# Graph attention on one core: slots of tile and row block in place of padded blocks, and 28 tiles fetched row by row by SyncE

## The reference

```
messages = x[col]
g = (messages @ W_gate.T + b_gate)[:, 0]
h = messages @ W_lin.T + b_lin
seg_max = segment_max(g, row)
e = exp(g - seg_max[row])
denom = segment_sum(e, row) + 1e-16
pooled = segment_sum((e / denom[row])[:, None] * h, row)
out = layernorm(x + pooled @ W_out.T + b_out)
```

## Time and profile before

| what | value |
|---|---|
| median of three runs | 2772.81 us |
| the profiled execution | 2774.84 us |
| its span, first to last instruction | 2773.0 us |
| mean granted TensorE clock | 0.604 of full speed |
| instructions | 24,827 |
| PE, DVE, ACT, POOL busy | 945.0, 1669.9, 147.0, 1746.0 us |

### The profile page before, as it was taken

How to read it: one execution, slowest core, us unless ns; L and a number is a source line. 1 busy time by engine, 2 the same in 40 slices (tenths; PEclk the granted TensorE clock), 3 DMA queues, 4 the chain that set the end, 5 groups by cost and what they waited for, 6 DMA issues and landing times.

```text
span 2773.0 us, 24827 instructions
## 1 busy us (share of the span) xinstructions
PE 945.0 (34%) x4932; PEld 799.1 (29%) x4932; DVE 1669.9 (60%) x5579; ACT 147.0 (5%) x489; POOL 1746.0 (63%) x1795
## 2 busy tenths in 40 slices
PE   6322110243342432433423424334234243342340
PEld 5311110232242332422423323323223233232230
DVE  9999997365464564654645646546455465464466
ACT  2311110000000000000000000000000000000006
POOL 0010004777777777777777777777777777777737
PEclk9655555566555565565656656556565565565665
DMA  3220002222222222222222222222222222222563
GB/s 121 95 80 0 0 0 55 54 54 54 54 54 55 54 55 54 54 55 54 54 55 54 55 54 54 55 54 54 55 55 55 54 54 55 54 54 55 47 29 93
DMA packets 91152, 148.65 MB, mean 54 GB/s; under 512 B 30551, under 2 KB 62127, under 8 KB 90495
## 3 DMA queue, kind: packets, MB, share of 16 engines
q0 software_dynamic: 56224, 117.06, 19.5%
q1 hardware_dynamic: 34032, 31.04, 3.3%
q10 hardware_dynamic: 864, 0.20, 0.1%
HBM read 134.35 MB, written 13.83 MB: 53 GB/s over the span
## 4 chain that ended last, share of the span: by engine, by line
POOL 33%; DVE 27%; issue 23%; PE 8%; DVEq 4%; DMA 3%; ACT 1%; ACTq 0%; POOLq 0%; SPq 0%
POOL arena L354 33%; DVE spread L875 5%; DVE nodes_sb L881 4%; PE bank L574 4%; DMA arena<-node_table,gather_at 3%; DVE rows_a L709 2%; DVEq L903 2%; DVE rows_b L710 2%; DVE rows_a L710 2%; DVE rows_b L709 2%; DVE turn_b L710 1%; PE bank L487 1%; DVE turn_b L709 1%; DVE turn_a L710 1%; DVE turn_a L709 1%
## 5 line engine op out<-in xcount | busy, mean ns | idle before, releaser
L354 POOL DMA_INDIRECT arena<-node_table,gather_at x1757 | 1681.0, 957 | 829.7 <-issue 527.2
L574 PE MATMUL bank<-arena,spread 128*128 128x129 f32 x3520 | 738.4, 379 | 323.3 <-DVE nodes_sb L881 220.2
L574 PEld LDWEIGHTS bank<-arena,spread 128*128 128x128 f32 x3520 | 643.4, 276 | 413.8 <-DVE nodes_sb L881 291.4
L875 DVE TENSOR_SCALAR spread<-iota_row,place_t,weights 128x128 f32<-128x128 f32 x1760 | 596.6, 355 | 174.0 <-PE bank L574 73.3
L881 DVE SCALAR_TENSOR_TENSOR nodes_sb<-nodes_sb,weights,bank 128x129 f32 x1760 | 605.4, 344 | 56.4 <-PE bank L574 11.2
L853 DVE TENSOR_TENSOR_SCAN run_max<-pen,bank 40x128 f32<-40x128 f32 (+1 forms) x45 | 18.5, 412 | 752.5 <-PE bank L556 752.5
L556 PE MATMUL bank<-ident,arena 128*40 128x128 f32 (+1 forms) x45 | 17.1, 380 | 703.2 <-DMA arena<-node_table,gather_at 703.2
L556 PEld LDWEIGHTS bank<-ident,arena 128*40 128x40 f32 (+1 forms) x45 | 5.3, 118 | 711.2 <-issue 711.2
L543 PE MATMUL bank<-ident,dst_f 40*128 40x40 f32 x44 | 13.1, 297 | 269.6 <-DVEq L684 269.6
L543 PEld LDWEIGHTS bank<-ident,dst_f 40*128 40x128 f32 x44 | 7.9, 179 | 279.3 <-issue 279.3
L533 PE MATMUL bank<-ident,rows_a 128*128 128x128 f32 x112 | 28.1, 428 | 153.2 <-DVE rows_a L735 117.9
(11 more groups left out here) (151 smaller groups left out, 993.0 us busy)
## 6 DMA issues: line engine op xcount, KB each, us to landing
arena<-node_table,gather_at POOLq DMA_INDIRECT x1757, 19.8
node_table<-arena SPq DMA_DIRECT2D x1, 6347.7 KB
nodes_sb<-in_x SPq DMA_DIRECT2D x4, 1562.5 KB
arena<-in_x SPq DMA_DIRECT2D x12, 448.0 KB
out<-arena SPq DMA_DIRECT2D x12, 448.0 KB
k<-sorted_keys SPq DMA_DIRECT2D x132, 20.0 KB
turn_a<-in_src SPq DMA_DIRECT2D x1, 828.0 KB
turn_b<-in_dst SPq DMA_DIRECT2D x1, 828.0 KB
```

What stands on the lines that cost most here:

```text
L354: pool.indirect_dma_start(out=gathered_rows[par][:, t, :], out_offset=None, in_=table[:, :], in_offset=bass.IndirectOffsetOnAxis(ap=gather ...
L574: last = pe.matmul(tile_ps(slot), lhsT=spread[:, slot, :], rhs=gathered_rows[par][:, b * BATCH + u, 0:WIDTH], start=True, stop=True)
L875: return dve.tensor_scalar(spread[:, slot, :], iota_row[:, :], place_t[par][:, t:t + 1], weights[par][:, 0, t:t + 1], ALU.is_equal, ALU.mult)
```

## The change

- **No padding.** The keys hold row and fetched node, and are sorted as they are: 1661 tiles (42 chunks, the last of 21 tiles). A tile may now span blocks. A **slot** is a pair of a tile and a block that it touches: 1661 + 97 = 1758 slots, in 44 rounds of 40. The counting, the one-hots and the pad keys go.
- **Tables ordered by PE.** Which tile a slot belongs to follows from counting how many tiles' ends lie before it: `find_ended` compares on DVE, PE sums over partitions, `place_slots` makes one-hot rows `chosen` and the register tables `pe_at` and `dve_at`, and PE multiplies `row_f` and `drop_x` of the last four chunks by `chosen` (`choose_rows`, `choose_drops`). Rows in a slot that belong to another block find no place and give zeros.
- **Weights on ACT.** `spread` holds only ones and zeros; ACT scales each fetched row by its weight, 40 instructions a chunk. PE takes the tile at an address from a register.
- **Ring.** Five chunk buffers, not two, since a round may still need a tile of three chunks before. All loops are written out.
- **SP fetches.** In chunks with c % 3 < 2, tile 32 is fetched by SP: 128 transfers of one row (28 such tiles). POOL leaves them out and issues 1633.
- **Moved.** The linear bias goes into the table by a bias matmul a batch. The copy of `blank_row` becomes `memset(sums, 0.0)`. x is loaded late, into sort buffers and two ring buffers, and POOL adds the bias behind its last gather. The constant 1e-16 is added before the reciprocal. The first two batches of spreads of a round stand ahead of its softmax. The last chunk isn't split.

The core of the diff, shortened:

```diff
-TILES = (EDGES + BLOCKS * (P - 1)) // P
+TILES = -(-EDGES // P)
+CHUNKS = -(-TILES // T)
+SLOTS = TILES + BLOCKS - 1
+ROUNDS = -(-SLOTS // T)
+RING = 5
+WINDOW = 4
+SP_TILE = 32
+ROW_LOADS = 16
...
+def by_sync(c):
+    return c % 3 < 2 and tiles_of(c) == T
...
+            def gather_tile(c):
+                if c >= RING:
+                    sp.wait_ge(tiles_summed, last_use(c - RING))
+                for p in range(0, P, ROW_LOADS):
+                    sp.nop(nofuse=True)
+                    got = nc.values_load_multi_w_load_instructions(
+                        sync_at[c % 2][SP_TILE:SP_TILE + 1, p:p + ROW_LOADS], engines=[ENGINE.SP], min_val=0,
...
+                    for k in range(ROW_LOADS):
+                        sp.dma_start(chunk_rows[c % RING][p + k:p + k + 1, SP_TILE, :],
+                                     table[bass.ds(got[k], 1), :]).then_inc(sync_gathered[sync_set(c)], 16)
+
+            for c in range(CHUNKS):
+                sp.wait_ge(k3_used, c + 1)
+                if c + 1 < CHUNKS:
+                    load_chunk(c + 1)
+                if by_sync(c):
+                    gather_tile(c)
...
-            pool.tensor_copy(sums.rearrange("p (b w) -> p b w", w=WIDTH),
-                             blank_row[:, :].unsqueeze(1).to_broadcast([P, BLOCKS, WIDTH])).then_inc(sums_blank, 1)
+            pool.memset(sums, 0.0).then_inc(sums_blank, 1)
...
+            for c in range(CHUNKS):
+                pool.wait_ge(prep_copied, c + 1)
+                if c >= RING:
+                    pool.wait_ge(tiles_summed, last_use(c - RING))
+                for t in range(tiles_of(c)):
+                    if by_sync(c) and t == SP_TILE:
+                        continue
+                    pool.indirect_dma_start(out=chunk_rows[c % RING][:, t, :], out_offset=None, in_=table[:, :],
...
+            def weigh(c):
+                act.wait_ge(expo_turned, c + 1)
+                act.activation(weights[c % 2][:, :], expo_ps, ACT.Exp).then_inc(weights_ready, 1)
+                keep_drops(c)
+                act.wait_ge(weights_ready, c + 1)
+                for t in range(-(-tiles_of(c) // BATCH) * BATCH):
+                    row = chunk_rows[c % RING][:, t, 0:WIDTH]
+                    last = act.activation(row, row, ACT.Copy, scale=weights[c % 2][:, t:t + 1])
...
+            for n in range(ROUNDS):
+                if n + 1 < ROUNDS:
+                    turn_prep(n + 1)
+                if n < CHUNKS:
+                    turn_softmax(n)
+                choose_drops(n)
+                if n + 1 < ROUNDS:
+                    choose_rows(n + 1)
+                sum_slots(n)
...
+            for n in range(ROUNDS):
+                if n + 1 < CHUNKS:
+                    prepare(n + 1)
+                if n + 1 < ROUNDS:
+                    find_ended(n + 1)
+                at = {}
+                add_slots(n, at, True)
+                if n < CHUNKS:
+                    softmax(n)
+                if n + 1 < ROUNDS:
+                    place_slots(n + 1)
+                if n < CHUNKS:
+                    dve.wait_ge(weights_ready, n + 1)
+                dve.wait_ge(drops_ready, n + 1)
+                add_slots(n, at, False)
+                if n + 1 < ROUNDS:
+                    find_places(n + 1)
```

More of the change, by code:

```diff
@@ L116, in graph_attention, with early_sb @@
         sums = nodes_sb[:, 0:BLOCKS * WIDTH]
[L117 to L125, removed]
+        ring = sb("ring", [P, RING * T * ROW])
+        node_rows = ring[0:NODE_ROWS, 0:NODE_COLS * ROW].rearrange("p (n f) -> p n f", f=ROW)
+        chunk_rows = [ring[:, k * T * ROW:(k + 1) * T * ROW].rearrange("p (t f) -> p t f", f=ROW) for k in range(RING)]
+        early = {}
+        early_at = NODE_COLS * ROW
+        def early_sb(width, rows=P):
+            start = early_at + sum(early.values())
+            early[start] = width
+            assert start + width <= RING * T * ROW
+            return ring[0:rows, start:start + width]
+        nodes_t = [early_sb(TURN * NODE_ROWS) for k in range(2)]
+        bg = sb("bg", [1, 1])
+        iota_i, iota_row = early_sb(P).bitcast(I32), sb("iota_row", [P, P])
         part_idx_i, part_idx = sb("part_idx_i", [P, 1], I32), sb("part_idx", [P, 1])
@@ new lines, in slot_values, with spread_slot @@
+            def slot_values(n, b):
+                many = min(2, batches_of(n) - b) * BATCH
+                got = nc.values_load_multi_w_load_instructions(
+                    dve_at[n % 2][0:1, b * BATCH:b * BATCH + many], engines=[mybir.EngineType.DVE],
+                    min_val=0, max_val=(BLOCKS - 1) * WIDTH, skip_runtime_bounds_check_because="a block times the width")[1]
+                return {b * BATCH + k: got[k] for k in range(many)}
+            def spread_slot(n, t, slot):
+                return dve.tensor_scalar(spread[:, slot, :], iota_row[:, :], places[n % 2][:, t:t + 1], None, ALU.is_equal)
@@ new lines, in add_slot, with add_slots @@
+            def add_slot(n, t, slot, at_col):
+                here = sums[:, bass.ds(at_col, WIDTH)]
+                dve.wait_ge(sums_added, slots_upto(n) + t + 2 * BATCH)
+                dve.scalar_tensor_tensor(here, here, drops[n % 2][:, t:t + 1], tile_ps(slot), ALU.mult, ALU.add).then_inc(sums_added, 1)
+            def add_slots(n, at, first_half):
+                end = batches_of(n)
+                for b in range(0, 2) if first_half else range(2, end + 2):
+                    if b < end and b % 2 == 0:
+                        dve.nop(nofuse=True)
+                        at.update(slot_values(n, b))
+                    if b >= 2:
+                        dve.wait_ge(tiles_summed, batches_upto(n) + b - 1)
```

592 lines of the change are left out of this document (277 added, 315 removed).

## The result

| | kernel before | changed kernel |
|---|---|---|
| median | 2773.22 us (2772.11 to 2774.74, 4 runs) | 2983.72 us (2978.50 to 2984.28, 4 runs) |
| ratio | 1 | 1.0756, interval 1.074 to 1.0772 |
| profiled execution, its span | 2774.84, 2773.0 us | 2984.28, 2982.5 us |

7.6% slower, where 2964 us and 6.8% were forecast.

The account below looks back on a forecast made before the run. POOL's gather issue bounds the kernel before; SP's closed turn was to bound the changed one. SP's start 428, thirteen turns and a tile pair to 2776.6, rounds 118.6, close 67.3, outside 1.84: 2964 us, overall range 2605 to 3030.

Parts of the forecast that it names:

- SP's closed turn: Gather stage: SP's two tiles wait on DVE's round through `prepare`; 2X + 39.1 = 170.3 us per three chunks, chance 0.44.
- first gather: Before the gathers: start moves from 445.5 to 414 us, 21 us from one-hots, counts and keys, 10 from the memset.
- row on SP: SP's one-row transfers: 0.469 us each, taken from the key loads; lower bound 0.34.
- register load of 16 values: SP's tile fetch: eight such loads a tile at about 0.7 us each, 5.6 us together.
- X: SP's time for one tile: 128 rows, 60.0 us, plus register loads, 5.6 us, giving 65.6 us.
- transpose to next `prepare`: DVE's share of a round, gate transpose to next `prepare`: from 30.8 to 33.6 us (31 to 37).
- rounds 40 to 43: Last four rounds, the final two without gathers to hide behind: 33.6 + 35 + 25 + 25 = 118.6 us.
- rival B: SP's rows at 0.408 us, X 57.8, turn 154.7 us: 2746 us, 1% faster; chance 0.12.
- the sign turns: SP's tile time at which slower becomes faster: X = 58.8 us, 0.416 us a row.
- the loss of cover: Table build on PE: if bias matmuls no longer lay beside DVE's sort phases, they would cost their own 20 to 30 us.
- The memset: Before the gathers: POOL's copy into `sums` becomes a memset, freeing a held-up DVE exchange; gain 0 to 10.3 us, 10 taken.
- own range: Whole time if SP's closed turn holds, X from 64 to 68 and DVE's share 31 to 37: 2915 to 3035 us.

Follow-up runs that it names:

- f1: Changed kernel with no tile fetched by SP, POOL issuing all 1661 gathers: 2742.03 us, ratio 0.9894 to the kernel before.
- f2: Changed kernel with DVE preparing chunk n+2 in the middle of round n, SP keeping its 28 tiles: 2771.30 us, ratio 1.0001 to the kernel before.
- e5: Changed kernel without the 34 bias matmuls, so the table lacks its bias: 2922.16 us, ratio 1.0542 to the kernel before.
- f3: Changed kernel with the bias matmuls over 128 rows, 127 of them zero, instead of one: 2927.12 us, ratio 1.0558 to the kernel before.
- e4: Changed kernel with 424 unused bf16 matmuls ahead of the table's build: 4665.17 us while the kernel before took 3779.25, ratio 1.2350.
- e1: Changed kernel with no tile fetched by SP, same edit as f1: 3940.47 us while the kernel before took 3779.25, ratio 1.0427.
- e3: Changed kernel with the early prepare, same edit as f2: 4448.37 us while the kernel before took 3779.25, ratio 1.1775.

## Why the prediction was right, and where it was only lucky

The kind, slower by SP's closed turn, and the size, 2964 against 2984, are right; that the size is so near is in part luck. By its own steps:

| step | predicted | measured |
|---|---|---|
| first gather | 414 | 467.6 |
| SP's tile 0 starts | 428 | 485.4 |
| row on SP | 0.469 us | 0.408 us |
| register load of 16 values | 0.7 us | 1.23 us |
| X, one tile, first load to last row | 65.6 us | 63.7 us; 64.9 from the first row of one tile to that of the next, with three key loads between |
| first add behind the transpose | 10.9 us | 11.5 us |
| transpose to next `prepare` | 33.6 us | 34.3 us |
| turn of three chunks | 170.3 us | 166.2 us, mean of 13 |
| gate transpose of chunk 40 | 2776.6 | 2774.7 |
| rounds 40 to 43 | 118.6 us | 140.6 us |
| close | 67.3 us | 67.1 us |

**The closed turn** is as described. f1 shows that SP's share makes it (241 us), f2 that the late `prepare` closes it: SP's waiting falls by 212 us, and the time by 211. The gate transposes of chunks 3k were released by SP's transfers, 14 times for 339.1 us, as the text said they would be. For those of chunks 3k+1 the profile names no releaser ("issue", 14 times for 357.5 us), but they too follow SP: the one at 1112.81 starts 1.4 us behind the end of SP's last row.

**The price of a row** was rival B's, 0.408, and not mine. The transfer itself takes 225 ns and not the 290 of the key loads, with both register instructions repeated. What kept B from coming true is the register load: I had 0.7 us from DVE's 0.596 for eight values; SP's sixteen take 1.23, twice as long for twice as many. The rows are 7.8 us a tile cheaper by their median, the loads 4.2 us dearer, and the first rows behind each load stand further apart than 0.408, some 1.6 us a tile; that leaves 1.9 us. With the measured X of 63.7 the text's own sum, 2X + 39.1, gives 166.5 us a turn for the 166.2 measured, far above the 148.6 of POOL. An X of 58.8, from which the sign turns, would have needed some 0.37 us a row beside such loads.

**The start of the gathers is the step that failed**: "The 34 bias matmuls added on PE lie beside the short phases of the sort on DVE; the table is wanted only when the gathers start." The table is, but PE is wanted at 92 us, when the short phases end, and PE takes its work in order: the sort's first transposes stood behind the build until 149. The text priced the loss of cover at the matmuls' own 20 to 30 us, and set it against the store and not against the transposes. They were busy for 55 us themselves and slowed the build around them. Where the cover holds, in e5 and f3, the first gather starts at 408.1 and 412.7: the 31 us forecast for the one-hots, the counts and the memset were there, 37.4 and 32.8 measured.

**The memset** gave its 10 us: beside it the exchanges took 0.55 to 0.69 us in the changed kernel. The Trainium skill (SBUF — State Buffer, "Who interferes with whom") let two-input DVE instructions pass beside a write, and names `tensor_scalar` among those that can take the shared port; both are in the trace, the second in f3, 4.6 us late.

**The end** is 22 us longer than the sum: the four rounds took 38.7, 39.6, 34.6 and 27.8 us for the 33.6, 35, 25 and 25 forecast. 6 us of the first are a DVE instruction held behind POOL's adds of x, 6.43 us for some 0.35 (L910 at 2777.01), and five spreads of 1.9 to 2.2 us, for 0.28 elsewhere, lie beside POOL's later adds. "The adds of x move to POOL behind its last gather, 14 times about 2 us, covered by these rounds" was right for POOL's time and left out DVE's. The rest of it, above all in round 42, was not taken apart.

**The sum** came out only 20 us off because errors cancel, and that is the luck in it. The prologue is 57 us late at SP's tile 0; the thirteen turns and the last pair give back 53 + 6 us, so that chunk 40's transpose is 2 us early; the last rounds add 22. Had the prologue gone as forecast, with all else as measured, the time would be near 2930 (f3, with its first gather at 412.7, measured 2927): inside the own range of 2915 to 3035, and 34 us below the forecast. That range is itself too narrow for what it names: both lower ends together, X of 64 and 31 us of DVE, give 2883 in the text's sum, both upper ends 3079; 2915 to 3035 is about what X alone does.

## What to carry to other kernels

Before work is given to an idle queue, write out what the queue waits for and who waits for it: 131 us of SP beside 149 of POOL looked free, and the tiles cost 241 us, since the next input came from the engine that waited for SP's output. Giving the input out half a round earlier (f2) was worth 211 us, not giving the work away at all (f1) 241. For work that is added "beside" something, look up the next instruction in the same engine's order, not the next user of its result.

## What the runs showed of the hardware that was not expected

**A matmul of one row slows its neighbours.** The granted clock reads 1.00 from 25 to 75 us in the changed kernel, in e4 and in f3 alike, which is the level of 2.4 GHz. Yet six of the same 128x129 matmuls take 1.65 us in the first two and 0.82 in f3, so here the granted clock doesn't show a factor of two that the matmuls' times do. The kernels differ in what else PE does in the build: with a bias matmul of one row in every batch it stays slow for all 126 us; with the same matmuls over 128 rows it is fast from 28 us on, without them from 27. 424 matmuls over all 128 rows ahead of the build (e4) did not carry over. Why one row does this no run shows.

**Issue on SP**: a one-row transfer with an address from a register costs 0.408 us of the queue, 0.225 of them the transfer instruction, the rest two register instructions and gaps. A load of sixteen register values takes 1.23 us there, one of eight 0.596 on DVE.

**A chain of adds on POOL can hold one DVE instruction over several of them**: 19.02 us behind nine adds, back to back, of 2.06 us each (f1), and 6.43 us over the rest of four (changed kernel). It need not be so: beside the five adds from 2811.03 to 2822.6 in the changed kernel two spreads in a row took 2.2 us each, and each ended with one add. What decides between the two, no run shows.

**At times all of these kernels ran a third slower or more**, with ACT instructions that wait for nothing 1.4 us apart: the kernel before 3779 us for 2772, the kernel without SP's tiles 3940 (e1) for 2742 (f1), the early prepare 4448 (e3) for 2771 (f2). Against the kernel before the ratio was then 1.04 without SP's tiles, 1.14 with one in three chunks and 1.24 with two (e4). The cause stays open.
